# Where TensorE waits for the transposed probabilities in the last slots of a four-layer graph kernel

## What is computed

```python
# layer 0: edge maximum
x = _layernorm(x + _L0_gnn_ref(x, adj, adj, L0_gnn_b), axis=-1)
# layer 1: graph attention (softmax of leaky_relu(s1 + s2) * adj, then att @ h, elu)
x = _layernorm(x + _L1_gnn_ref(x, L1_gnn_W, L1_gnn_a, L1_gnn_beta, adj), axis=-1)
# layer 2: adj @ x @ weight + bias
x = _layernorm(x + _L2_gnn_ref(x, adj, L2_gnn_weight, L2_gnn_bias), axis=-1)
# layer 3: attention with 8 heads of 64
    q = (x @ Wq + bq).reshape(b, n, H, HD)
    k = (x @ Wk + bk).reshape(b, n, H, HD)
    v = (x @ Wv + bv).reshape(b, n, H, HD)
    scores = jnp.einsum('bihd,bjhd->bhij', q, k) / jnp.sqrt(jnp.float32(HD))
    scores = scores + mask[None, None, :, :]
    weights = jax.nn.softmax(scores, axis=-1)
    out = jnp.einsum('bhij,bjhd->bihd', weights, v)
```

## Time and profile before

| | |
|---|---|
| median of 3 runs | 2584.06 us (2577.85 to 2586.65) |
| the profiled execution, its own time | 2577.72 us |
| its span, first to last instruction | 2575.9 us |
| PE busy | 2443.8 us, 95% |
| DVE busy | 2209.0 us, 86% |
| POOL, ACT busy | 56%, 51% |
| PEclk of the execution | 0.98 |

### The profile page before, as it was taken

One profiled execution on the slowest core, in us unless ns is written; L12 is line 12 of the kernel. 1 busy time (PEld: TensorE's weight loads), 2 busy tenths in 40 slices (PEclk: granted clock), 3 DMA queues, 4 the chain that ended last, 5 costly groups with the idle time before them and its releaser, 6 DMA issues. The chain is left out here.

```text
span 2575.9 us, 54890 instructions
## 1 busy us (share of the span) xinstructions
PE 2443.8 (95%) x15501; PEld 2075.4 (81%) x15501; DVE 2209.0 (86%) x6954; ACT 1324.9 (51%) x4096; POOL 1443.9 (56%) x1793
## 2 busy tenths in 40 slices
PE   5899999999999999999999999999999999999654
PEld 3688888888888888888888888888888888888543
DVE  6898999899899989989998998999999899999432
ACT  3455555555555555555555555555555555555221
POOL 2466665665666666566565656656565665656211
PEclk9999999999999999999999999999999999999876
DMA  4366666656666665666566566656656665665332
GB/s 128 74 136 143 140 138 141 144 129 147 139 139 138 140 144 128 147 140 140 137 141 144 129 146 141 140 135 142 144 129 145 142 140 136 141 144 119 74 80 72
DMA packets 1375067, 340.98 MB, mean 132 GB/s; under 512 B 1078576, under 2 KB 1339312, under 8 KB 1375024
## 3 DMA queue, kind: packets, MB, share of 16 engines
q1 hardware_dynamic: 1375024, 340.47, 58.0%
HBM read 173.35 MB, written 166.99 MB: 132 GB/s over the span
## 5 line engine op out<-in xcount | busy, mean ns | idle before, releaser
L1796 PE MATMUL rot<-w_hi,y_hi 128*128 128x512 f32 x1024 | 415.2, 405 | 4.7 <-DVE y_lo L1708 3.4
L1798 PE MATMUL rot<-w_hi,y_lo 128*128 128x512 f32 x1024 | 403.3, 394 | 0.0
L1797 PE MATMUL rot<-w_lo,y_hi 128*128 128x512 f32 x1024 | 402.0, 393 | 0.0
L756 ACT ACTIVATE probs<-score,sc_nmax 128x128 f32<-128x128 f32 x1024 | 361.2, 369 | 42.8 <-DVE sc_nmax L1132 39.2
L482 POOL TENSOR_TENSOR ve<-mv,eps_col 128x1 f32<-128x1 f32 (+1 forms) x448 | 129.2, 289 | 401.7 <-DVE mv L1117 303.1
L590 POOL TENSOR_TENSOR x2b<-x,bias 128x512 f32<-128x512 f32 x120 | 155.8, 1299 | 243.6 <-DVE x L1450 243.6
L1132 DVE CUSTOM_DVE_ANT_0 score<-score,mask 128x128 f32<-128x128 f32 x1024 | 259.4, 315 | 0.0
L490 POOL TENSOR_TENSOR rs<-ve,half_neg 128x1 f32<-128x1 f32 (+1 forms) x448 | 251.5, 575 | 1.0
L1151 DVE CUSTOM_DVE_ANT_0 dot_tmp<-x,u 128x512 bf16<-128x512 f32 x256 | 234.7, 953 | 4.8 <-ACT x L869 0.4
L1796 PEld LDWEIGHTS rot<-w_hi,y_hi 128*128 128x128 f32 x1024 | 193.8, 189 | 54.7 <-DVE y_lo L1708 3.9
L1851 PE MATMUL rot<-xt,wq_hi 128*128 128x512 f32 x512 | 200.1, 423 | 32.7 <-DMA probs_t<-pt_hbm 32.7
(11 more groups left out here) (242 smaller groups left out, 6936.4 us busy)
## 6 DMA issues: line engine op xcount, KB each, us to landing
pt_hbm<-probs SPq DMA_DIRECT2D x508, 128.0 KB, 2.8
probs_t<-pt_hbm SPq DMA_DIRECT2D x127, 512.0 KB, 4.0
x_in<-in_x SPq DMA_DIRECT2D x128, 256.0 KB, 4.0
xt_hbm<-x_b SPq DMA_DIRECT2D x512, 64.0 KB, 2.4
xt_f<-xt_hbm SPq DMA_DIRECT2D x128, 256.0 KB, 2.8
out_x<-x SPq DMA_DIRECT2D x128, 256.0 KB, 2.4
ot_hbm<-o_t SPq DMA_DIRECT2D x508, 64.0 KB, 1.9
o_norm<-ot_hbm SPq DMA_DIRECT2D x127, 256.0 KB, 2.7
```

What stands on the lines that cost most here:

```text
L756: ins = act.activation(probs[:, 0, c, t, :], score_tile(c, g, h), ACT.Exp, bias=sc_nmax[:, c, t:t + 1], scale=-1.0, accum_out=sc_sum[:, pa ...
L1796: pe.matmul(outp, lh, rh, start=first, stop=False)
L1797: pe.matmul(outp, lh, rl, start=False, stop=False)
L1798: return pe.matmul(outp, ll, rh, start=False, stop=last)
```

## The change

In TensorE's `drain` the block that waits for the transposed probabilities (with the last graph's transposes in its other branch) moves from the head of the slot to the place directly in front of the products with the values. Everything that stood between the two places is unchanged and keeps its order. A wait for `score_exp` of the slot before is added in front of the scores of the last graph, in all three functions; only `drain` ever reaches that case (slot 133). The other engines' functions are untouched.

```diff
             def drain(slot):
-                if slot.on(L_PV):
-
-                    if slot.last(L_PV):
-                        ... (waits and transposes of the last graph)
-                        pe.wait_ge(last_pt_done, 2)
-                    else:
-                        slot.wait(pe, pt_in, L_PV, each=16)
                 if slot.on(L_GAT):
...
                     slot.wait(pe, q_done, L_QK)
                     slot.wait(pe, k_done, L_QK)
+                    if slot.last(L_QK):
+                        slot.wait(pe, score_exp, L_QK, 1)
                     for c in range(CHUNKS):
...
                     projection(late_k_bank, "wk", slot.after(), True).then_inc(k_mm, 1)
                 if slot.on(L_PV):
+
+                    if slot.last(L_PV):
+                        ... (waits and transposes of the last graph)
+                        pe.wait_ge(last_pt_done, 2)
+                    else:
+                        slot.wait(pe, pt_in, L_PV, each=16)
                     first = slot.buf(L_PV, BUFS) // GROUP * GROUP
```

More of the change, by code:

```diff
@@ L2194, in drain @@
                 if slot.on(L_PV):
+                    if slot.last(L_PV):
+                        pe.wait_ge(r2_done, GRAPHS)
+                        pe.wait_ge(z0_done, GRAPHS)
+                        for h, bank in enumerate((rot[1], s2_bank)):
+                            if h == 0:
+                                pe.wait_ge(half_exp, 1)
+                            else:
+                                slot.wait(pe, score_exp, L_PV)
+                            for c in range(CHUNKS):
+                                for g in range(GROUP):
+                                    at = (c * GROUP + g) * P
+                                    ins = pe.transpose(bank[:, at:at + P], probs[:, 0, c, g * 2 + h, :], ident[:, :])
+                            ins.then_inc(last_pt_mm, 1)
+                        pe.wait_ge(last_pt_done, 2)
+                    else:
+                        slot.wait(pe, pt_in, L_PV, each=16)
                     first = slot.buf(L_PV, BUFS) // GROUP * GROUP
```

## The result

The changed kernel takes 2518.51 us (median of 4 runs, 2516.93 to 2520.15), the kernel before beside it on the same chip 2584.91 us (4 runs, 2577.85 to 2586.65). The ratio is 0.9748, with a 95% interval of 0.9729 to 0.9768: 66.4 us less by the medians. The profiled executions differ by 59.0 us (2577.72 and 2518.76). The forecast was 2521 us in a range of 2511 to 2534.

What follows compares the result with a forecast made beforehand. In the drain a chain of waits sets the pace, with transfer and PE's block in series. Slot gains of 12.9 + 10.9 + 12.4 + 11.1 + 13.8 + 1.8 = 62.9 us take 2584.06 to 2521, range 2511 to 2534.

Steps and rivals of the forecast that it cites:

- The circle: Drain slots: exponentials, transpose, scatter, gather, PE's block, products with the values, VectorE, next exponentials in series; at most 66.9 us to win.
- something else anchors: Rival, slots 128 to 132: input's and output's memory trips collide in SyncE's queue, 4 us each; 2541 us, chance 0.11.
- It does nothing: Rival, whole drain: the circle runs through something beside PE equally slow; time within 0.3% of before, chance 0.03.
- slower: Rival, drain: PE's instruction supply cannot keep pace without the long waits; 2592 us or more, chance 0.03.
- the six terms: Gains forecast for slots 128 to 133: 12.9, 10.9, 12.4, 11.1, 13.8 and 1.8 us.
- the term of 1.8 us: Slot 133: only the scores, 2.01 us, run early; products with the values then at lower clock, 1.97 us, not 1.73.
- The term that was off: Slot 132: a 12.9 us block against a 12.74 us wait, sticking out 0.5 with slack; gain 13.8 us.
- Its wait for the input's low part: Slot 132: the first projection must wait for the input's low part, ending 0.7 us after PE is free.
- The lower clock: Rival, drain: half of the block stays at 1.2 GHz, so gain is 54.7 us and time 2529; chance 0.15.
- all near clock 1.0 up to slot 132: Expected profile: slot 129 about 20 us, slots 130 and 131 about 19 and 15, clock near 1.0 up to slot 132.
- The term of slot 131: Slot 131: a 9.7 us block, its scores at the lower clock, against a 9.37 us wait; gain 11.1 us.
- The rule on transfers side by side: Slots 128 and 129: a 3.07 us scatter would delay the landing as much, giving 2524 us; forecast kept 0.45 us instead.

Runs made afterwards that it cites:

- the doubled gather: The changed kernel with the gather of the transposed probabilities made twice in a row in slots 128 to 133, the second counted; 2543.65 us.
- the repeat: The changed kernel run again with no edit, for a second profile; 2519.76 us, ratio 0.9757 to the kernel before.
- the best kernel: Changed kernel plus slot 133's probabilities transposed on TensorE, VectorE's sums there behind its masked minima, unread products in slots 128 and 131; 2506.57 us, ratio 0.9711 to before.
- the fillers in slots 130 to 132 of before: The kernel before, wait still at the slot's head, with 40, 36 and 50 unread products ahead of it in slots 130, 131 and 132; 2577.50 us.

## Why the prediction was right

**The circle.** The prediction said that transfer and block stood in series without need. With the wait behind the query projection a part of the block was covered and a part of the gain came, 13.6 us, and the doubled gather showed that the transfer still closes the circle. Its rival "something else anchors" wanted 4 us more in each slot; the rows have 0.84 and 0.65 us of waiting for the transfer in slots 130 and 132, none in 128, 129 and 131 (in the repeat 0.41 in 128 and 0.35 in 131), and none for layer 3's input among PE's longest. "It does nothing" and "slower" fell with the result; the instruction supply did not hold PE up in slots that are now full (18.01 of 20.0 us in slot 129).

**The terms.** The blocks of slots 128 and 129 took 11.50 and 11.29 us (2419.34 - 2408.05) where 11.4 had been added up from full-pace rows. Five of the six terms hold within 0.3 us, and slot 130 waits 0.84 us for the landing, where its term has 1.1 (a block of 9.5 us against 10.60). The last scores' new wait shows no cost, as said. In slot 133 the old 11.76 us have split into 2.34 for the exponentials, 1.16 for the scores and 8.26 for the landing: the products with the values stand at the end of the same trip, and only the scores left it. The lower clock that the term of 1.8 us counts shows behind those products: slot 133 gained 2.0, and the rest took 0.2 us longer.

**The term that was off** is slot 132: 13.8 forecast, 12.5 measured. The forecast let the block alone set its end and took the transfer's old length. Measured, PE waited 0.65 us for the landing, with the scatter 1.8 us longer than before; and the block started 1.4 us late, because the products for the values v of slot 131 ran at the lower clock: their twelve records take 3.98 us from the first start to the last, those of slot 132 2.59 (PE, slot 131):

```profile
2459.43 0.76 PE L1796 MATMUL rot<-wv_hi,xt 128*128 128x512 f32 x1 [0.91 <-DVE o_t L1690]
```

Its wait for the input's low part, 0.7 us in the sum, did not come: PE started the block without idle time. Both the slow scatter and the slow products are gone in the best kernel, and there the slot takes 18.55 us, 1.9 less than in the changed kernel; the forecast implies 32.95 - 13.8 = 19.15. How the two share the 1.9 was not measured apart.

**The lower clock.** The rival was that it would stay in the drain and leave a gain of 54.7 us. It was wrong in its size: at the blocks' heads the clock is full, in slots 128 to 132. It was right that it would not go everywhere, and my line "all near clock 1.0 up to slot 132" was wrong: slot 131 reads 0.80, where its scores wait for the queries (2.38 us), and took 16.7 us, not 15. The term of slot 131 had been put with a low clock for the scores and held; what the low clock did to the products for the values behind them fell on slot 132.

**Against the median.** The sum gave 2521 against a median of 2584.06; 2518.51 was measured. The drain's own gain is 62.0 us in the traces and 61.1 on the chip that ran both again; 66.4 in the first comparison was more than that because before's runs there had a high median: 2584.91 of 4, where the longer series beside the later runs have 2580.85 to 2581.95. The 2584.06 that the forecast started from was some 2.6 us high in the same way, so most of the 2.5 us between 2521 and 2518.51 is the base and not the gain.

**The rule on transfers side by side.** The Trainium skill, in DMA: Bandwidth & Descriptors (Rules for kernel authors), says of two transfers to disjoint partition halves that they serialize, since both use the same 16 DMA engines. The prediction took that for any two transfers side by side; the sum would have been 59.6 us. SyncE of after, slot 128:

```profile
2392.49 0.38 SPq L326 DMA_DIRECT2D probs_t<-pt_hbm  x1
2393.16 2.69 SPq L322 DMA_DIRECT2D xt_hbm<-x_b  x4
```

PE starts the products with the values at 2396.74, 4.25 us behind the gather's issue, and does not wait for it. A landing pushed out by the scatter's 2.69 us would be at 3.94 + 2.69 = 6.63. In the repeat PE did wait there, 0.41 us, and started 4.29 us behind the gather's issue (2401.78 - 2397.49), so the landing came at most about 0.35 us later than the 3.94 alone. The traces do not bear out the rule, taken that widely, for these two transfers: slots 128 and 129 gained 12.9 and 11.2 us.

## What to carry to other kernels

Read which instruction stands behind a wait, not only what is waited for: on an engine that serves in order, a wait one place too early holds back everything up to its true reader, here 10 to 13 us of products, with the short waits between them, in each of five slots. The gain is the part of the block that fits into the wait, plus what the lower clock behind the wait had cost, and it is added up slot by slot from starts, since the next bound comes close behind: here the block and the landing end within 2 us of each other in slots 128 to 132. Measure a change at the end of a long kernel by the stretch that it touches: here it repeats within 2 us while the 2,385 us ahead of it wander by 7.

## What the runs showed of the hardware

**A wait of 1.4 to 3 us can be followed by the lower clock, and its length alone does not decide.** A row of slot 128 of after: a wait of 2.96 us, and then records of 0.63 to 0.70 us for the 0.39 of full clock.

```profile
2400.79 0.35 PE L2224 MATMUL att_bank<-ident,att_n 128*128 128x128 f32 x1 [2.96 <-DVE att_n L1717]
2400.89 0.70 PE L1796 MATMUL rot<-w_hi,y_hi 128*128 128x512 f32 x1
```

The same waits stand in nearly all of the twelve executions, and what follows them differs:

- 2.96 us, slot 128: records of 0.63 us in nine of the ten executions that have it; with the wait behind the queries they were 0.47 and then 0.39.
- 2.38 us, slot 131: the scores took 1.16 us (full clock) with the doubled gather, 1.50 in after, 1.88 in before, 2.08 with the fillers in slots 130 to 132 of before.
- 1.99 us, slot 129: 0.50 and then 0.40 or 0.39 in ten (in two of these 0.63 from the seventh record on), 0.80 and then 0.63 with the doubled gather and in the best kernel.
- 1.39 us, slot 130: 0.50 and then 0.40 or 0.39 in ten, 0.79 and then 0.63 with the doubled gather and with the wait moved in slot 130 alone.

What decides it is not shown here. Eleven unread products in the 2.96 us wait kept the records at 0.47 and 0.39, and the slot from there to the next products with the values took 21.01 instead of 22.40 us; but in that same kernel the clock fell in slot 129, and slot 130 took 20.00 instead of 19.25.

**Instructions come in by the same DMA engines.** While this straight-line code runs, the trace has a queue of instruction loads: single packets of 0.02 MB, of 0.9 to 1.6 us on one engine. They are TensorE's by one sign: with 56 more instructions on TensorE the load near slot 132's scatter came at 2464 instead of 2467. Where one fell into a scatter of small packets (533 under 512 B in that microsecond), the scatter took 6.6 to 7.0 us instead of 5.1, in four executions; that it is the cause is supported only. If it is, a change in the number of instructions ahead of a transfer can cost or give back 1 to 2 us with no other reason in the code.
